# A second attention's queries computed with tokens over partitions, normalised there and turned by DMA, in a two-block transformer kernel

## The reference, cut to what matters

```
h = layernorm(x)
q = (h @ Wq.T)  -> 32 heads of 128          k, v = ctx @ Wk.T, ctx @ Wv.T -> 8 heads of 128
q = q_norm_w * q * rsqrt(mean(q*q) + eps)   k = k_norm_w * k * rsqrt(mean(k*k) + eps)
scores = q @ k.T / sqrt(128) + mask         (each of 8 k/v heads serves 4 query heads)
x = x + (softmax(scores) @ v) @ Wo.T
```

## Time and profile before

| | us |
|---|---|
| median of 3 runs | 2441.4 (2441.06 to 2441.74) |
| the profiled execution's own time | 2442.63 |
| its span, first to last instruction | 2440.8 |
| PE busy | 2371.1 (97%) |
| DVE, ACT, POOL busy | 1635.9, 1254.0, 1223.9 |
| attention 1, units 0 to 31 | from 1406.7 to some 2357.7 |

### The profile page before, as it was taken

The page is one execution under the profiler, slowest core; times in us unless marked ns, Lnnn a source line. Parts: engine busy times, 40 slices in busy tenths (PEclk is TensorE's granted clock), DMA queues, the critical chain, the costliest instruction groups (busy, mean ns, idle before and its releaser), DMA issues.

```text
span 2440.8 us, 45008 instructions
## 1 busy us (share of the span) xinstructions
PE 2371.1 (97%) x17656; PEld 1293.2 (53%) x17664; DVE 1635.9 (67%) x3133; ACT 1254.0 (51%) x2425; POOL 1223.9 (50%) x981
## 2 busy tenths in 40 slices
PE   7799999999999999999999999999999999999998
PEld 4455555555555555444444555555555555555554
DVE  7877777777777788755443556667666666755666
ACT  7665655555565554423232554555455555544453
POOL 3556666666666666323222355544444455445531
PEclk9899999999999999999999999999999999999999
DMA  6111121212121111111100111122221212221101
GB/s 209 44 36 34 48 52 34 53 27 53 27 53 27 42 40 27 35 28 51 35 19 12 44 31 27 27 62 59 47 61 36 61 36 62 52 43 27 27 14 69
DMA packets 216753, 108.13 MB, mean 44 GB/s; under 512 B 169280, under 2 KB 192480, under 8 KB 216544
## 3 DMA queue, kind: packets, MB, share of 16 engines
q1 hardware_dynamic: 216544, 105.25, 17.5%
HBM read 61.62 MB, written 4.19 MB: 27 GB/s over the span
## 4 chain that ended last, share of the span: by engine, by line
PE 54%; DVE 4%; POOL 3%; ACT 1%; issue 1%; DVEq 0%; ACTq 0%; POOLq 0%
PE PB L859 14%; PE PB L811 12%; PE PB L971 9%; PE PB L795 6%; PE PB L988 5%; PE PB L836 2%; PE PB L901 2%; PE PB L880 1%; DVE SML L1927 1%; PE PB L1085 1%; DVE AR L2116 1%; PE PB L930 1%; POOL AR L2729 1%; POOL PSP L2708 0%; POOL AR L2690 0%
## 5 line engine op out<-in xcount | busy, mean ns | idle before, releaser
L859 PE MATMUL PB<-WB,AR 128*128 128x512 f16 x3072 | 692.5, 381 | 19.5 <-DVE X L2131 12.6
L811 PE MATMUL PB<-XTB,WB 128*128 128x512 f16 x3072 | 677.9, 379 | 3.4 <-ACT WB L1357 2.0
L859 PEld LDWEIGHTS PB<-WB,AR 128*128 128x128 f16 x3072 | 296.3, 98 | 384.5 <-DVE X L2131 24.1
L811 PEld LDWEIGHTS PB<-XTB,WB 128*128 128x128 f16 x3072 | 297.2, 98 | 346.1 <-issue 3.1
L2701 POOL TENSOR_TENSOR AR<-AR,SML 128x512 f32<-128x512 f32 x128 | 144.6, 1151 | 317.1 <-DVE SML L2101 317.1
L2131 DVE SCALAR_TENSOR_TENSOR X<-PB,SML,X 128x512 f32<-128x512 f32 x256 | 187.4, 748 | 162.4 <-PE PB L859 156.2
L1481 ACT ACTIVATE AR<-PB 128x512 f16<-128x512 f32 x256 | 131.6, 598 | 238.2 <-PE PB L901 238.1
L2690 POOL TENSOR_TENSOR AR<-AR,CST 128x512 f32<-128x512 f32 x128 | 182.9, 1429 | 40.1 <-ACT AR L1391 40.1
L2011 DVE TENSOR_TENSOR AR<-PB,AR 128x512 f16<-128x512 f32 x128 | 88.2, 690 | 168.0 <-ACT AR L1444 168.0
L971 PE MATMUL PB<-XTB,AR 128*128 128x512 f16 (+1 forms) x864 | 192.5, 379 | 0.0
L1982 DVE TENSOR_TENSOR AR<-AR 128x512 f16<-128x512 f32 x128 | 138.6, 1084 | 71.1 <-ACT AR L1397 70.7
(11 more groups left out here) (272 smaller groups left out, 3778.4 us busy)
## 6 DMA issues: line engine op xcount, KB each, us to landing
STG<-in_wo SPq DMA_DIRECT2D x14, 1024.0 KB
STG<-in_wq SPq DMA_DIRECT2D x13, 1024.0 KB
STG<-in_qw_gu SPq DMA_DIRECT2D x40, 128.0 KB
STG<-in_ctxT SPq DMA_DIRECT2D x4, 1024.0 KB
X<-in_x SPq DMA_DIRECT2D x4, 1024.0 KB, 10.6
out_x<-X SPq DMA_DIRECT2D x16, 256.0 KB, 2.4
STG<-in_wk SPq DMA_DIRECT2D x14, 256.0 KB
STG<-in_wv SPq DMA_DIRECT2D x14, 256.0 KB
```

The lines of the kernel that those rows point to most:

```text
L811: m = pe.do.matmul(b[:, :], wq[x][:, k, h * 128:(h + 1) * 128], XT[y][c][:, k, :], start=n == 0, stop=n == 11)
L859: m = pe.do.matmul(b[:, :], AT[x][:, h, t * 128:(t + 1) * 128], wo[y][:, h, :], start=n == 0, stop=n == 11)
```

## The change

Only attention 1 changes.

- Queries: the stationary operand is now 128 tokens and the moving one the weights, so that step `t` gives 128 tokens over partitions and the 4 heads along the row. ACT squares the bank, DVE sums each head's 128 squares (`sums_1`), scales and adds eps, POOL raises 4 columns to -1/2 (`power_1`), DVE multiplies the bank by it (`queries_1`) and so empties the bank, ACT makes the high half, POOL (t = 0, 1, 2) or DVE (t = 3) the low one. Two tiles' halves lie side by side, and SP turns two tiles by two DMA transposes (64 partitions x 2048 each), so four a unit are added.
- `norm_q` and its 32 matmuls, the bf16 squares, and one of the two passes over the scores are gone. All keys are turned by DMA, and the first unit's softmax too.
- Order: TensorE does the four queries right behind the scores, then keys and values, then the outputs, in banks 4, 5, 2, 3. On the other engines the keys' and values' steps come last in the front. `plan_prep` is as it was; slots 0 to 4 keep their places among TensorE's query steps and get new places on DVE, ACT and POOL.

```
-        QB, WB_OUT, PVB = (0, 1, 6, 7), (2, 3, 0, 2), ((0, 1), (6, 7))
+            return ((4, 5, 2, 3) if L and u < NU - 2 else (2, 3, 0, 2))[t]
...
-        TB_R, TB_A, TB_LG, TB_W = (2, 2, 7), (3, 3, 1), (6, 6, 4, 1), (1, 2, 4)
+        TB_R, TB_A, TB_LG, TB_W = (2, 2, 7), (3, 3, 1), (4, 4, 4, 1), (1, 2, 4)
...
             # sync
+            def turn_q(u, two):
+                for t in (2 * two, 2 * two + 1):
+                    sp.wait_ge(q_hi, (1, u, t))
+                    sp.wait_ge(*halved(u, t))
+                if u > 0:
+                    sp.wait_ge(s_mm, (1, u - 1, 1))
...
+                for odd in range(2):
+                    sp.do.dma_start_transpose(out=QT_rows[:, odd, 2 * two:2 * two + 2, :].rearrange("p t (a q) -> p (t a) q", a=8),
+                                              in_=QHP[two][64 * odd:64 * odd + 64, :]).then_inc(qt_in.of((u, two), 16), 16)
...
+                        turn_p_pair(1, u, 0)
+                        turn_q(u + 1, 0)
+                        turn_p_pair(1, u, 1)
+                        turn_q(u + 1, 1)
                         turn_k(u + 1)
...
             # tensor: one query step, and the front
+            def queries_1(u, t):
+                b = bank(QB[t], (q_mul, (u, t)))
...
+                        m = pe.do.matmul(b[:, :], XT[x][c][:, k, t * 128:(t + 1) * 128], wq[y][:, k, :],
+                                         start=n == 0, stop=n == 11)
...
             def scores(L, u):
-                if k_by_dma(L, u):
+                if L:
                     pe.wait_ge(kt_in, u)
+                    pe.wait_ge(qt_in, (u, 1))
...
-            def norm_q(u):
-                bk = bank(5, (q_ms, u))
...
-                elif u > 1:
-                    keys_values(u, 0)
+                side(L, beside, 0)
+                for n in range(4):
+                    (queries_1 if L else queries_0)(u, n)
+                    side(L, beside, 1 + n)
+                if L:
+                    if u > 1:
+                        keys_values(u, 0)
                     keys_values(u, 1)
...
             # scalar: front
+                    squares_1(u, 0)
+                    exponent(1, beside)
+                    squares_1(u, 1)
+                    side(1, beside, 0)
+                    queries_1(u, 0)
+                    side(1, beside, 1)
+                    squares_1(u, 2)
+                    halved_p(1, beside)
+                    queries_1(u, 1)
+                    side(1, beside, 2)
+                    squares_1(u, 3)
+                    queries_1(u, 2)
+                    side(1, beside, 3)
+                    queries_1(u, 3)
+                    side(1, beside, 4)
+                    if u > 1:
+                        values_1(u, 0)
+                    values_1(u, 1)
+                    halved_k(u)
...
             # vector
+            def sums_1(u, t):
+                g, rs = UNITS[1][u][0], RSQ[:, 4 * t:4 * t + 4]
+                dve.wait_ge(q_sq, (u, t))
+                dve.do.tensor_reduce(rs, M1[t].rearrange("p (h d) -> p h d", h=4), AX, ALU.add).then_inc(q_sum.of((u, t)), 1)
+                dve.wait_ge(q_sum, (u, t))
+                dve.do.tensor_scalar(rs, rs, 1.0 / DH, eco(1, g, 0), ALU.mult, ALU.add).then_inc(q_ms.of((u, t)), 1)
+
+            def queries_1(u, t):
+                dve.wait_ge(q_pow, (u, t))
...
             def front(L, u, beside):
...
+                    sums_1(u, 0)
+                    soft_sum(1, beside)
+                    queries_1(u, 0)
+                    for t in range(1, 4):
+                        sums_1(u, t)
+                        side(1, beside, t - 1)
+                        queries_1(u, t)
+                    side(1, beside, 3)
+                    low_1(u, 3)
+                    side(1, beside, 4)
+                    if u > 1:
                         values_1(u, 0)
-                        soft_sum(1, beside)
-                        values_1(u, 1)
...
             # gpsimd: front
+                    power_1(u, 0)
+                    soft_norm(1, beside)
+                    side(1, beside, 0)
+                    power_1(u, 1)
+                    queries_1(u, 0)
+                    side(1, beside, 1)
+                    halved_p(1, beside, 0)
+                    power_1(u, 2)
+                    queries_1(u, 1)
+                    side(1, beside, 2)
+                    halved_p(1, beside, 1)
+                    power_1(u, 3)
+                    queries_1(u, 2)
+                    side(1, beside, 3)
+                    side(1, beside, 4)
                     keys_1(u)
+                    halved_k(u)
```

More of the change, by code:

```diff
@@ L1143, in front @@
                         values(u)
-                elif u > 1:
-                    keys_values(u, 0)
+                side(L, beside, 0)
[5 more added lines that the diff above has]
+                        keys_values(u, 0)
                     keys_values(u, 1)
-                side(L, beside, 0)
-                for h in range(4):
-                    queries(L, u, h)
-                    side(L, beside, 1 + h)
             def units(L):
@@ L1272, in tensor @@
             keep_warm(12, 0)
[L1273 to L1274 removed]
+            queries_0(0, 0)
+            queries_0(0, 1)
             peak(w(0, 1, 0), 5)
[L1276 to L1277 removed]
+            queries_0(0, 2)
+            queries_0(0, 3)
             keys(1)
@@ L1295, in tensor @@
             keys_values(0, 1)
-            down(*FFN[-1])
+            for t in range(4):
+                queries_1(0, t)
             ln_turn(2, 1, 1)
-            for h in range(4):
-                queries(1, 0, h)
+            down(*FFN[-1], (2, 3))
             keys_values(1, 0)
-            turn_k(0)
-            keys_values(1, 1)
-            norm_q(0)
+            down(*FFN[-1], (0, 1))
             units(1)
@@ L1846, in scalar @@
             values_1(0, 1)
+            for t in range(4):
+                squares_1(0, t)
+                if t == 0:
+                    halved_k(0)
+                else:
+                    queries_1(0, t - 1)
             ln_turn(2, 1, 1)
-            for h in range(4):
-                queries_1(0, h)
-            keys_1(0)
+            queries_1(0, 3)
+            values_1(1, 0)
             act.do.activation(TBL, CST[:, 0:1], ACTF.Exp).then_inc(t_act.of("table"), 1)
@@ L2643, in vector @@
             values_1(0, 1)
-            down(*FFN[-1])
+            for t in range(4):
+                sums_1(0, t)
+                if t > 0:
+                    queries_1(0, t - 1)
+            queries_1(0, 3)
             ln_low(2, 1, 1)
-            for h in range(4):
-                queries_1(0, h)
-            keys_1(0)
-            norm_q(0)
+            low_1(0, 3)
+            down(*FFN[-1], (2, 3))
+            values_1(1, 0)
+            down(*FFN[-1], (0, 1))
             units(1)
@@ L2819, in units @@
                     for slot in range(5, 9):
-                        if L and slot == 7:
-                            norm_q(u + 1)
                         side(L, u, slot)
@@ L2874, in gpsimd @@
             keys_1(0)
-            for h in range(4):
-                queries_1(0, h)
-            norm_q(0)
+            for t in range(4):
+                power_1(0, t)
+                if t == 0:
+                    halved_k(0)
+                else:
+                    queries_1(0, t - 1)
             units(1)
```

284 lines of the change are left out of this document (106 added, 178 removed).

## The result

The changed kernel takes **2627.4 us** (median of 4 runs, 2627.2 to 2628.2) against 2441.5: a ratio of 1.0761, 95% interval 1.0747 to 1.0774. The forecast was 2618, with 2585 to 2660 for the likeliest case: slower, by 186 us where 176.5 were worked out. Of those 186 the profiled execution shows 184.6 inside its span (2625.4 less 2440.8).

The account below looks back on a forecast made before the run. TensorE, busy 97% of the span, was taken to bound the kernel, so new waits count in full. Differences 111 - 2 + 8.5 + 21 + 14 + 13 + 11 = +176.5 us, including the 25.9 saved, gave 2618 us, range 2585 to 2660.

Parts of the forecast that it names:

- the likeliest case: Forecast of 2618 us taken together with slow transposes, range 2585 to 2660; chance 0.64.
- The saved matmuls: TensorE's norm matmuls go: 32 units x 0.81 = 25.9 us, all on the path.
- The bank wait: Preparing iterations: keys and values half 1 waits for bank 3, free at 19.8 instead of 14.45, so 5.35 us.
- +111: Total added over 17 preparing iterations: 13 x 6.65 + 4 x 6.1 us, clock charge included.
- What sets 19.8: POOL's queue, 9.5 us from first normalisation at 9.35 to 18.85, then DVE's multiplication 0.68 and peak reduce 0.28.
- The clock: Each new TensorE wait lowers the granted clock for matmuls behind it: 2.2 us charged, bounds 0 and 3.4.
- the first rival: The clock stays up after TensorE's new waits: 2618 - 50 = 2568 us; chance 0.2.
- Iterations 2, 4, 25, 27 to 30: Bank 2/3 waits from slot work: 2, 4 +6.5 us each; 25 +8.5; 27, 29 +10.5 each; 28, 30 +7 each.
- The plain iterations: Iterations 3, 11, 15, 19, 26, without a peak: 29.35 us each through the keys' chain, -2 in all.
- the wait is about half the difference: Plain iterations: keys' transpose lands 29.8 to 30.4, scores due 28.8; starting later than DVE, they wait only 0.6 us.
- Costed at nothing: Four added transposes a unit on SP, 1.23 us each, landed by 26 before scores due at 28.8; also weight loads, output banks.
- Rival 4: Transposes are slow on SP's one queue, landing 3 us later: 2625 to 2650 us; chance counted within the forecast's 0.64.

Follow-up runs that it names:

- the filler run: Changed kernel plus 15 filler matmuls between the two halves of keys and values in the 17 preparing iterations: 2596.3 us, ratio 1.0634.
- the run with the power first: Changed kernel with POOL's fourth power moved ahead of the softmax's second low half: 2607.5 us, ratio 1.0679.
- the run with DVE's order changed: Changed kernel, bank 3 kept, with DVE's slot 3 (the peak's reduce) ahead of its fourth multiplication: 2576.6 us, ratio 1.0559.

## Why the prediction was right, point by point

- **The saved matmuls**, 0.81 an iteration: right. The kernel before without most of them is 23 us shorter; only 28 of 32 go there, and 28/32 of 25.9 is 22.7.
- **The bank wait** carries the forecast, and one edited bank number removes it. Bank 3 free at 19.8: measured 19.76 on average over the 17. The average hides a spread, 18.0 to 22.3: iterations 12, 16 and 20 were read as 0.55 earlier than the rest and are 1.5 to 2.1 earlier, 5 was counted with them and isn't early (19.5), 8 and 24 are late (22.3 and 21.7). That +110.6 stands against +111 is in part luck. The wait of 5.35 came out as 4.4 at that line because more stands between: the peak waits for ACT in 9 iterations (0.6 at most), and in some the first query step waits for banks, as below. Seen as a start of the second half, 19.8 against 14.45, it is right.
- **What sets 19.8**: right in the sum, by two errors that cancel, and incomplete in the mechanism. The first normalisation was put at 9.35 and starts at 8.92 on average. POOL's queue from there was counted as 9.5 us without a gap and takes 9.86: it has gaps of 0.1 for DVE, whose scaling, left out of my list as one small operation, takes 0.9 beside POOL. Without the scaling the queue is 9.42 and the start 0.17 earlier, 0.6 us an iteration together.
- **The clock**, charged at 2.2 with bounds 0 and 3.4: 2.08 by the filler run. 19.76 and 14.50 make 34.3, and with the clock it is the 36.3 that was measured; the first rival (2568) fell.
- **Iterations 2, 4, 25, 27 to 30**: the waits that were read are there, and other slots and banks gave 40.6 us back, all of the loss in 2, 4, 28 and 30 but a third and under a half of it in 27, 29 and 25. Sizes were off. 2 and 4 were 3.9 too small together: the turns' banks are free at 21.1 and 20.0, as read, but TensorE comes to them late (a wait of 3.8 and not 5), because the turns' matmuls themselves wait 2.0 for ACT, and the first query step 1.9 and 0.7 for `weigh`'s bank; so iteration 2 has 7.8 us without TensorE's work. In 25 the wait behind the set-up is 5.5 and not 8; 2.1 at the first query step and the clock (48 query matmuls in 12.21 us instead of 10.52) bring it to +9.7. 27 and 29 were 3.7 too large: `t_turn` waited 5.2, not 5.9, and the clock cost about 1.1 behind it (12 matmuls in 3.81 us instead of 2.75).
- **The plain iterations** failed: 30.4, not 29.35, so +3.6 instead of -2. The step at fault is "the wait is about half the difference". The landing of 29.8 to 30.4 was nearly right (the scores start 30.0 to 30.6 behind the last ones), and the scores wait for all of it.
- **"Costed at nothing"**: the transposes cost 1.24 to 2.62 us of SP each, not 1.23, and yet SP was idle before the keys' one. Rival 4's cause was wrong. What delays the scores is the keys' chain, which the reading of the plain iterations had; in preparing ones it shows only once the bank is free, 22.3 us in 15 waits.
- **Not in the forecast**: the first query step waits for `weigh`'s bank where DVE is late (L848 <- L2135, 9.3 us in 6 waits, in iterations 2, 4, 8, 25, 27 and 29), and 2.2 us come before and after the loop. The 8 us between 176.5 and 184.6 are +5.6 (plain), +3.9 (2 and 4), +2.2 (outside the loop), -3.7 (27 and 29), and small ones.

## What to carry to other kernels

When a block is moved in a hand-ordered schedule, list for every bank that moved work writes who empties it and what that reader now stands behind; a side job with a 0.2 us matmul cost 100 us here because its reader followed the longest chain of the iteration. Price each new wait of a saturated TensorE as the wait plus the matmuls behind it at the lower clock (2.08 us on average here, behind 3.0 to 5.4 us idle). And take out the wait that heads the list in a run of its own: what comes up behind it (here the keys' chain) tells what the new order is worth at its best.

## What the runs showed of the hardware that was not expected

- DVE's `tensor_scalar` on 4 float32 columns takes 0.23 us in the 22 cases of iterations 3 to 24 in which POOL is idle, and 0.83 to 1.02 in the 66 beside a running POOL instruction, ending 0.02 to 0.03 behind it; with 3 columns it is the same, with one column it isn't held up at all. The reduce (0.68) and the product from a bank (0.69) don't grow. Another operation does: DVE's low half of the queries, with two inputs in SBUF (L2045), takes 0.67 to 0.69 with POOL idle and 1.18 to 1.37 in the run with the power first, ending 0.55 behind a difference on POOL in all 22. The kernel before had a case too, in the keys' scaling of 4 columns: 0.48 us in iterations 3 to 24 beside POOL (L2003), 0.22 in the changed kernel with POOL idle (L2028). By the Trainium skill (GPSIMD Engine Reference, 8. Key points) POOL shares its SBUF interfaces with VectorE and contends with its two-port modes and its instructions with two SBUF inputs, and `tensor_scalar` can run in such a mode (VectorE: DVE Perf Modes, Mode 2×_2P — use both read ports for one tensor); this trace agrees for three and four columns (0.83 to 1.02 us instead of 0.23), and shows besides that this wait lasts to the end of POOL's instruction.
- The price of one gap isn't fixed. In the run with DVE's order changed, seven iterations have the second half of the keys and values start 3.02 us behind the start of the matmul before it, 2.75 of them idle. In one of them (6) the rest of the iteration takes 14.50 us, as at full clock, in the others (7, 10, 14, 18, 22, 23) 15.83 to 16.23. What decides isn't shown. In iterations 8, 12, 16 and 20 of the same run the idle time is 1.2 to 1.6 us, and the rest takes 14.50 each time.
